# A two-layer transformer block: output projection, LayerNorm and layer 1 projections in one block, layer 1 score products in three places of a step

## What is computed

```python
x = hidden_states
xn = _layernorm(x)
x = x + L0_attn(xn) + L0_ffn(xn)      # latent attention, 32 heads, top 128 keys; out @ o_w at its end
xn = _layernorm(x)                    # (x - mean) / sqrt(var + 1e-5)
x = x + L1_attn(xn) + L1_ffn(xn)

# L1_attn: H, G, HD = 32, 8, 16; four query heads share one key/value group
q  = (x @ Wq).reshape(b, t, H, HD)
kv = (x @ Wkv).reshape(b, t, G, 2, HD)
scores  = where(causal, -inf, q @ k.T)
weights = softmax(scores / sqrt(HD))
out = (weights @ v) @ Wo + bo
```

## Time and profile before

| | us |
|---|---|
| median of 3 runs (lowest, highest) | 1913.16 (1911.1, 1920.36) |
| time of the profiled execution | 1918.64 |
| its span in the trace | 1916.5 |
| PE busy in the span | 1723.9 (90%) |
| DVE, ACT, POOL busy | 1073.1, 855.7, 705.5 |

### The profile page before, as it was taken

How to read it: one execution, slowest core, us unless ns; L and a number is a source line. 1 busy time by engine, 2 the same in 40 slices (tenths; PEclk the granted TensorE clock), 3 DMA queues, 4 the chain that set the end, 5 groups by cost and what they waited for, 6 DMA issues and landing times. The chain is left out here.

```text
span 1916.5 us, 27661 instructions
## 1 busy us (share of the span) xinstructions
PE 1723.9 (90%) x8954; PEld 1253.4 (65%) x8954; DVE 1073.1 (56%) x2460; ACT 855.7 (45%) x1607; POOL 705.5 (37%) x744
## 2 busy tenths in 40 slices
PE   6889995999959999999999998994779898879999
PEld 5578884887847666666666664773645444448887
DVE  3436668999147777677767773225255666600122
ACT  3545653443225555555555553432114555553321
POOL 1201113444635666566655562651101121125221
PEclk9899997999969999999999999996758999989999
DMA  8820002221010000000000001542702233122111
GB/s 243 267 80 22 22 11 67 67 58 31 25 35 1 30 17 16 16 16 31 16 16 16 31 12 45 197 132 47 171 1 46 53 66 73 30 76 89 34 50 50
DMA packets 106231, 110.43 MB, mean 58 GB/s; under 512 B 38656, under 2 KB 69856, under 8 KB 106112
## 3 DMA queue, kind: packets, MB, share of 16 engines
q1 hardware_dynamic: 102016, 101.58, 19.5%
q10 hardware_dynamic: 4096, 7.34, 1.1%
HBM read 81.34 MB, written 27.39 MB: 57 GB/s over the span
## 5 line engine op out<-in xcount | busy, mean ns | idle before, releaser
L1895 DVE CUSTOM_DVE_ANT_0 ga_sm<-ps,strip 128x640 f32<-128x640 f32 (+7 forms) x256 | 186.6, 756 | 124.7 <-PE ps L1812 123.1
L1268 POOL TENSOR_SCALAR a_p<-a_p,a_rinv 128x640 f32<-128x640 f32 (+7 forms) x256 | 191.1, 750 | 174.2 <-DVE a_rinv L1194 173.1
L1225 ACT ACTIVATE a_p<-a_sm,a_nmax 128x640 f32<-128x640 f32 (+7 forms) x256 | 198.5, 776 | 106.2 <-DVE a_nmax L1186 103.3
L1186 DVE CUSTOM_DVE_ANT_0 a_sm<-ps,maskb 128x640 f32<-128x640 f32 (+7 forms) x256 | 192.7, 753 | 91.7 <-PE ps L1130 88.0
L1915 ACT ACTIVATE ga_pt<-ps 128x1024 f32<-128x1024 f32 (+1 forms) x192 | 149.4, 811 | 122.4 <-PE ps L1835 121.8
L1142 PE MATMUL ps<-ident,a_p 128*128 128x128 f32 x1152 | 173.2, 276 | 12.2 <-DVE a_pt L1201 11.9
L1812 PE MATMUL ps<-ga_kst,ga_qst 96*128 96x512 f32 (+3 forms) x384 | 125.4, 414 | 44.4 <-DVE ga_nmax L1895 34.9
L1142 PEld LDWEIGHTS ps<-ident,a_p 128*128 128x128 f32 x1152 | 133.6, 141 | 35.0 <-DVE a_pt L1201 11.2
L1954 POOL TENSOR_SCALAR_AFFINE_SELECT ga_pt<-ga_pt 128x512 f32<-128x512 f32 x64 | 40.7, 636 | 312.2 <-ACT ga_pt L1915 312.2
L1157 PE MATMUL ps<-a_pt,vst 128*64 128x512 f32 (+3 forms) x768 | 150.8, 502 | 1.8 <-DVE a_pt L1201 1.1
L1237 ACT COPY a_pt<-ps 128x512 f32<-128x512 f32 x128 | 74.3, 580 | 164.6 <-PE ps L1142 109.4
(11 more groups left out here) (274 smaller groups left out, 4024.5 us busy)
## 6 DMA issues: line engine op xcount, KB each, us to landing
op_wo<-in_L_attn_o_w SPq DMA_DIRECT2D x16, 512.0 KB, 6.4
ctx_d<-a_ctxst SPq DMA_DIRECT2D x16, 512.0 KB, 3.0
o_cr<-ctx_d SPq DMA_DIRECT2D x32, 256.0 KB, 3.0
o_wr<-wvo_d SPq DMA_DIRECT2D x32, 256.0 KB, 3.2
ga_qst<-qkd SPq DMA_DIRECT2D x48, 128.0 KB, 5.0
f_wr<-in_L_ffn_w SPq DMA_DIRECT2D x20, 256.0 KB, 2.5
op_wq<-in_L_attn_q_b_w SPq DMA_DIRECT2D x16, 288.0 KB, 4.9
x<-in_L_attn_hidden_states SPq DMA_DIRECT2D x16, 256.0 KB, 4.1
```

The costliest lines, as they stand in the source:

```text
L1186: dve.tensor_tensor_reduce(out=sm[kind][:, 0:w], in0=slots[kind][:, 0:w], in1=maskb[:, MASK_OFF[t]:MASK_OFF[t + 1]], scale=-scale, scalar= ...
L1225: act.activation(p[kind][:, v // 2 % 2, 0:w], sm[kind][:, 0:w], ACT.Exp, bias=nmax[:, v % 4:v % 4 + 1], scale=-1.0, accum_out=rsum[:, v % ...
L1268: pool.tensor_scalar(mine, mine, rinv[:, v % 4:v % 4 + 1], 1.0, ALU.mult, ALU.mult).then_inc(norm_done, 1)
L1895: dve.tensor_tensor_reduce(out=sm[kind][:, 0:w], in0=slots[kind][:, 0:w], in1=strip[:, S - w:], scale=-1.0, scalar=3.0e38, op0=ALU.add, op ...
```

## The change

`project_out`, `layernorm` and `layer1_qkv` are replaced by one function, `outputs_to_queries`, in one block; the barriers and `Ctx.begin`s between them go, its semaphores are started with those of the enclosing scope (62 in all, where `project_out` started 24) and not marked finished at its end, and its loops are written out. The bias matmuls are gone (the first real one starts the bank). Layer 1's weight blocks are loaded and split between steps of the projection (`LOAD_AT`, `SPLIT_AT`), POOL sets `v32` and `kst` after steps 5 and 7 of half 0, DVE its part of `kst` ahead of step 0. Half 0's LayerNorm runs between the steps of half 1: adds at steps 2 and 3, statistics at 4 and 5, `Sqrt` at 6, normalising from 7, PE's turns after steps 8 to 11, ACT's copies at 9 to 12, DVE's low parts at 10 to 13. Then come 5 T tasks of half 0 (half 1's tiles are turned after the fourth), 4 V tasks of half 0, 5 T and 4 V tasks of half 1, in a ring of 4 banks. T results are stored as halves (20 stores of 256 KB where there were 10 of 512 KB). The buffers of the projection lie in those of later steps. In `grouped_attention` the units of a step are put in three places: after keys 0, after keys 1, and after weigh.

```diff
...
+def outputs_to_queries(nc, c, ps, ident, x, ctx_d, wvo_d, xnh, xnl, wq, wkv, qkd, v32, ctxn, raw, sums, qst, kst, q_in,
+                       k_in):
+
+
+    NS = 4
+    NK = H // 2
     NQ = D // P
     NT1 = NQ + 1
     KD = G1 * HD1
+    NW = D + 2 * KD
+    BLOCKS = [NQ] + list(range(NQ)) + [NQ + 1]
+    LOAD_AT = {(0, 4): 0, (0, 6): 1, (0, 8): 2, (1, 0): 3, (1, 2): 4, (1, 4): 5}
+    SPLIT_AT = {(0, 8): 0, (0, 10): 1, (0, 12): 2, (1, 4): 3, (1, 6): 4, (1, 8): 5}
+    ROOT_AT, TURN_AT, HIGH_AT, LOW_AT = 6, 8, 9, 10
+    LANDED = [16 * DT, 16, 16, 16 * DT + 16, 32, 16 * DT + 16]
+    tasks = [("T", m, 0) for m in (NQ, 0, 1, 2, 3)] + [("V", t, 0) for t in range(4)]
+    tasks += [("T", m, 1) for m in (NQ, 0, 1, 2, 3)] + [("V", t, 1) for t in range(4, ST)]
+    TURNED = 4
+    lows = [n for n, task in enumerate(tasks) if task[0] == "T"]
...
+        norm = [raw[:, 0], raw[:, 1], sums[:, 0, 0:HALF], sums[:, 0, HALF:]]
...
+        ch, cl, oh_w, ol_w = four(oh, 0), four(oh, 2), four(ol, 0), four(ol, 2)
+        cr, wr = four(ctxn, 0), four(ctxn, 2)
...
+                for half, k, s, u in steps:
+                    if u:
+                        sp.wait_ge(cl_done[s], START + u)
+                        sp.wait_ge(wvl_done[s], START + u)
+                    sp.dma_start(cr[:, s], ctx_d[k][:, half * HALF:(half + 1) * HALF]).then_inc(raw_in[s], 16)
+                    sp.dma_start(wr[:, s], wvo_d[k]).then_inc(raw_in[s], 16)
+                    if (half, k) in LOAD_AT:
+                        load_block(LOAD_AT[half, k])
+                for n, i in enumerate(lows):
+                    _, m, h = tasks[i]
+                    at = slice(h * HALF, (h + 1) * HALF)
+                    sp.wait_ge(lo_done, START + n + 1)
                     for l, o in enumerate((oh, ol)):
+                        sp.dma_start(qkd[l][m * P:(m + 1) * P, at], f32(o[:, m, at])).then_inc(stored[m], 16)
+                    if (m, h) == (0, 1):
                         sp.wait_ge(zero_a, START + 2)
                         sp.wait_ge(zero_b, START + 3)
+                        sp.wait_ge(stored[NQ], START + 64)
+                        sp.wait_ge(stored[0], START + 64)
                         load_group(sp, qkd, qst, kst, q_in, k_in, 0)
+                    if (m, h) == (1, 1):
                         load_group(sp, qkd, qst, kst, q_in, k_in, 1)
+                sp.wait_ge(stored[1], START + 64)
...
+                for half, k, s, u in steps:
+                    pool.wait_ge(split_done[s], START + u + 1)
+                    pool.tensor_tensor(ol_w[:, s], wr[:, s], f32(oh_w[:, s]), ALU.subtract).then_inc(wvl_done[s], 1)
+                    if (half, k) in SPLIT_AT:
+                        low_block(SPLIT_AT[half, k])
+                    if (half, k) == (0, 5):
+                        pool.memset(v32[:, :, :, HD1:], 1.0).then_inc(ones_done, 1)
+                    if (half, k) == (0, 7):
+                        pool.memset(f32(kst[:, :, 1]), 0.0).then_inc(zero_b, 1)
+                        pool.wait_ge(zero_b, START + 1)
+                        pool.memset(f32(kst[KQ1:KQ1 + 2, :, 1]), 1.0).then_inc(zero_b, 1)
+                        pool.wait_ge(zero_b, START + 2)
+                        pool.memset(f32(kst[KQ1:KQ1 + 1, :, 1]), 0.0).then_inc(zero_b, 1)
+                        pool.wait_ge(zero_b, START + 3)
...
+                for half, k, s, u in steps:
+                    act.wait_ge(raw_in[s], START + (u + 1) * 32)
+                    if u:
+                        act.wait_ge(used[s], START + u)
+                    act.copy(ch[:, s], cr[:, s])
+                    act.copy(oh_w[:, s], wr[:, s]).then_inc(split_done[s], 1)
+                    if (half, k) in SPLIT_AT:
+                        high_block(SPLIT_AT[half, k])
+                    if half and k == ROOT_AT:
+                        root(0)
+                    if half and HIGH_AT <= k < HIGH_AT + 4:
+                        high_x(k - HIGH_AT)
+                for n in range(len(tasks)):
+                    high(n)
+                    if n == 1:
+                        root(1)
+                    if n == TURNED - 1:
+                        for t in range(4, ST):
+                            high_x(t)
...
+                def add(t):
+                    dve.wait_ge(used[NS - 1], START + (t // 4 + 1) * NK // NS)
+                    dve.tensor_tensor(x[:, t], ps[:, t, :], x[:, t], ALU.add).then_inc(x_done, 1)
...
+                for half, k, s, u in steps:
+                    dve.wait_ge(split_done[s], START + u + 1)
+                    dve.tensor_tensor(cl[:, s], cr[:, s], f32(ch[:, s]), ALU.subtract).then_inc(cl_done[s], 1)
+                    if half == 0:
+                        continue
+                    if k in (2, 3):
+                        add(2 * (k - 2))
+                        add(2 * (k - 2) + 1)
+                    if k == 4:
+                        measure(0)
+                    if k == 5:
+                        variance(0)
+                    if k == 7:
+                        invert(0)
+                    if 7 <= k < 11:
+                        normal(k - 7)
+                    if LOW_AT <= k < LOW_AT + 4:
+                        low_x(k - LOW_AT)
+                for t in range(4, ST):
+                    add(t)
+                measure(1)
+                variance(1)
+                low(0)
+                invert(1)
+                normal(4)
+                normal(5)
+                low(1)
+                low(2)
+                normal(6)
+                normal(7)
+                for t in range(4, ST):
+                    if t == 6:
+                        low(3)
+                    low_x(t)
+                for n in lows[4:]:
+                    low(n)
...
+                def task(n):
+                    kind, m, h = tasks[n]
+                    if n == 0:
+                        pe.wait_ge(wl_done, START + len(BLOCKS))
+                        pe.wait_ge(xl_done, START + 4)
+                    if h == 1 and tasks[n - 1][2] == 0:
+                        pe.wait_ge(xl_done, START + ST)
+                    if n >= 4:
+                        pe.wait_ge(hi_done, START + n - 3)
+                        pe.wait_ge(lo_done, START + len([i for i in lows if i <= n - 4]))
...
+                for half, k, s, u in steps:
+                    pe.wait_ge(cl_done[s], START + u + 1)
+                    pe.wait_ge(wvl_done[s], START + u + 1)
+                    for t in range(4):
+                        at = slice(t * P, (t + 1) * P)
+                        ins = mm3(pe, ps[:, 4 * half + t, :], (ch[:, s, at], cl[:, s, at]), (oh_w[:, s], ol_w[:, s]),
+                                  k == 0, k == NK - 1)
+                    ins.then_inc(used[s], 1)
+                    if half and TURN_AT <= k < TURN_AT + 4:
+                        turn(k - TURN_AT)
+                for n in range(len(tasks)):
+                    task(n)
+                    if n == TURNED - 1:
+                        for t in range(4, ST):
+                            turn(t)
...
                         done += SHARE[s]
                         keys(g, s, 0)
-                        for v in units[:len(units) // 2]:
+                        one, two = (len(units) + 1) // 3, (len(units) + 1) // 3 + len(units) // 3
+                        for v in units[:one]:
                             score(ahead, v)
                         keys(g, s, 1)
-                        for v in units[len(units) // 2:]:
+                        for v in units[one:two]:
                             score(ahead, v)
                         if s == NSTEP - LEAD and g + 1 < G1:
                             turn(g + 1)
                         if g * NSTEP + s >= LAG:
                             weigh((g * NSTEP + s - LAG) // NSTEP, (g * NSTEP + s - LAG) % NSTEP)
+                        for v in units[two:]:
+                            score(ahead, v)
...
```

## The result

The changed kernel takes 1867.46 us as a median of 4 runs (1865.87 to 1869.85), the kernel before beside it 1912.13 (1906.71 to 1920.36): a ratio of 0.9755, 95% interval 0.973 to 0.978, or 44.7 us less. The forecast of 1876 was 37 us less. The profiled execution took 1868.59 us with a span of 1866.5; that of before had 1918.64 and 1916.5, so the two spans differ by 50.0, 5 more than the medians, because the profile of before lies 5.5 above its median.

A forecast was written before the change was run, and what follows sets the result against it. The bound was PE with its waits for DVE, and between stages only latency. Terms of -25.3, -12.7 and +1.0 summed to -37.0 us: 1881.6 profiled, 1876 as a median, within a range of 1860 to 1895.

The forecast's parts named there:

- the early clock: Group 0, rival: PE's clock rises at the group's start, 33.4 for 48.15 us, about 14 less, 1862; chance 0.11.
- Beginning: Start of the projection: semaphores +1.2 us, dropped bias gains 0.6; first product at 1201.1 for 1200.45.
- Half 0: Projection's first half: 16 steps of 2.72 us and 3.0 for slow clock kept; PE waits 2.3 for POOL's settings.
- Half 1: Projection's second half: bias and slow clock go, turns add 2.2 us, waits 1.4; ends at 1297.0 for 1296.1.
- The ring's waits: Half 1: PE waits 0.1 to 0.6 us at three of five steps, 1.4 in sum (0 to 4).
- the clock and the seam: Between the halves: 3.69 us of second bias go, and the 3.5 us at 0.53 behind it, worth 1.6.
- The turns did not drop the clock: Half 1, rival: four turns drop the clock, half of it at 1.2 GHz, 22 us more, 1898; chance 0.03.
- Between: Projection to scoring: the 33.6 us go; order of tasks and stores is late next; block ends at T0 + 54.2.
- The three terms: Joined block up to the scoring stage: the next stage starts at 1352.1 for 1377.4, -25.3 us.
- Order of units: Groups 1 to 6: weigh runs in PE's idle time, period 33.4 for 35.6 us, -2.2 a group, -12.7 in all.
- Group 0: First group: PE at 1.2 GHz is busy 37.04 of 38.3 us and leaves nothing to fill, gain 0.
- End: End of the kernel: 17 more semaphore clears an engine, about 0.06 us each, +1.0.

The follow-up runs named there:

- values_late: Changed kernel with the five Q and K tasks of half 1 ahead of all value tasks: 1865.1 us, ratio 0.974 to before.
- single-part kernels: Changed kernel with the old order of units, 1895.77 us; kernel before with only the new order of units, 1892.98 us.
- best: Changed kernel with half 1's Q and K tasks first, POOL's settings spread, root tile's copies a step later, extra products after group 0's units: 1856.02 us.
- no_bias: Kernel before with its steps written out and without the bias products: 1921.39 us in one run.

## Why the prediction was right, point by point

The 1867.46 us lie within the range of 1860 to 1895, but just outside the 1868 to 1884 that the forecast itself was given: what came true is the forecast and, on top of it, part of the early clock, a rival at 0.11. Here are the terms one by one.

**Beginning: right.** The first product comes 13.14 us after the store of layer 0, for 12.45: +0.7, forecast +0.65 from 1.2 for the semaphores and -0.6 for the bias, which came to 0.5 alone.

**Half 0: right.** POOL's settings and PE's wait behind them, in the kernel after:

```profile
1214.28 2.66 POOL L1512 MEMSET ga_kst<- 128x3072 f32 x1
1217.00 2.66 POOL L1514 MEMSET ga_kst<- 2x3072 f32 x1
1219.71 2.66 POOL L1516 MEMSET ga_kst<- 1x3072 f32 x1
...
1222.46 1.26 POOL L1506 TENSOR_TENSOR oq_ol<-ctxn,oq_ol 128x512 fp32r<-128x512 f32 x1
```

```profile
1223.86 0.47 PE L105 MATMUL ps<-oq_ol,oq_oh 128*128 128x512 f32 x1 [1.76 <-POOL oq_ol L1506]
```

1.76 us there (1.77 to 2.47 in five other profiles of it or near it), for 2.3.

**Half 1: the sum right, one cause wrong.** The ring's waits are 0.46, 0.44 and 0.26 us, 1.2 for 1.4, with POOL as releaser; from the first product to the first task it is 95.85 us, for 95.9. That the clock and the seam cost 5.3 us held, that the bias was the whole reason did not: behind the bias lay the wait for DVE's in-order add, and a kernel that drops the bias alone pays 3.18 us of waiting in its place.

**The turns did not drop the clock.** PE ran the four turns of half 1 (0.60 us each) at a granted clock of 1.00, and the sixteen transposes ahead of half 1's tasks as well (two rows of eight, 1.03 and 1.04 us).

**Between: right.** First load at T0 + 30.5 for 31.8, first score product at + 54.5 for 55.1, idle PE 14.63 for 15. The three terms come to -26.0 for -25.3. values_late showed the named cause, the order of tasks and stores, to be the right one.

**Order of units: right and 16% too small.** -14.7 for -12.7, a period of 33.46 for 33.4. The mechanism is in the step shown above: weigh runs in the wait for a maximum, and the next keys follow 0.7 us earlier. One reading was off: I had PE idle for 1.0 us in that step, where the row has 0.74. Five groups gave 2.3 us each where the steps had 2.2; the sixth, the last with units ahead, gave 3.4 (35.70 to 32.27), where I had taken 0.5 off. Why it gives more stays open.

**Group 0: the step that failed.** I had put 0 there and the early rise of the clock among the rivals at 0.11, with up to 14 us if it came at the start of the group. It came about half-way, at 20 us for 42, and gave 8.8, which is what the result lies below the forecast (44.7 for 37.0, with the end's loss against it). That the result is still in the range is owed to the range's width, not to the sum. The step took the clock of before as given for a group whose instruction order was changed. It is the order, as the two single-part kernels show, and not certain to the us: in ten profiles with the new order the rise came 15 to 21 us after the group's start in eight and 34 in two, in three with the old order 42 or 43 in all.

**End: +3.2 for +1.0.** The semaphore clears at the very end (line view, the clears of the last 11 us: engine, count, ns, first and last start) are 29 on POOL over 2.0 us, where the kernel before had 12 over 0.8:

```profile
L73 POOLq EVENT_SEMAPHORE_RANGE_CLEAR  x29: 44/44/44, 1863.9 to 1865.9; - x29
```

From the issue of the first of the eight output DMAs to the end of the span it is 10.4 us for 8.6, which is 1.8 of the 3.2. I had 0.06 for each of 17 clears, 1.0. Of the rest 0.8 lies ahead of the first product of the feed-forward stage, whose weights' POOL half comes later, and why it does stays open. The remaining 0.6 lies in the feed-forward stage, whose beginning falls in a stretch at a granted clock of 0.50 that lasts 14 us in this trace and 10 before. The size isn't firm either: the other merged kernels have 240.7 to 244.1 us for this stretch, the old block 239.9 to 241.3.

## What to carry to other kernels

Before a filler that looks useless is taken out, look at what the in-order queues behind it do meanwhile: here 3.7 us of bias products lay over a wait of 3.2, and the gain came only in the kernel that also moved the add. When blocks are joined, follow the last item that the next stage needs through its stores and loads, and put it first: the order of ten short tasks was worth 6 us more of that stage. Count the clock of a stretch as unknown when the order of its instructions changes, and give it both values in the range.

## What was not expected of the hardware

The granted clock of a stretch did not follow from PE's busy time in it. In the first scoring stage it was 0.50 over 36 us with PE busy 22.3 us and also with 34.45; in group 0 PE was busy for 15.4 of the first 18 us in the changed kernel, and the rise to 2.4 GHz came after 15 to 21 us in eight profiles with the new order of units and 42 in three with the old. Adding products that should keep PE busy made the rise later twice (34 us), and not in two other kernels with the same additions. It fell back to 1.2 GHz in the middle of later groups, while PE was full: twice for over 20 us in the profile of values_late, at about 9 us each, twice for 10 us in that of best, at about 4, and once for 10 us in that of no_bias, which has the old order. What decides this stays open.
